# First attention: three VectorE steps move behind the next row's maxima, one ScalarE step moves ahead of two copies

## The reference, cut to what matters

```python
def _L0_xattn_ref(hidden_states, memory_tokens, memory_mask):     # (4,256,256), (4,1601,256), (4,1601)
    scores = jnp.einsum('bsd,bmd->bsm', hidden_states, memory_tokens) * scale
    scores = jnp.where(memory_mask[:, None, :], scores, neg_inf)
    attn = jax.nn.softmax(scores, axis=-1)
    readout = jnp.einsum('bsm,bmd->bsd', attn, memory_tokens)
    valid_b = jnp.any(memory_mask, axis=-1)
    return jnp.where(valid_b[:, None, None], readout, jnp.zeros_like(readout))
...
x = x + _L0_xattn_ref(_layernorm(x, axis=-1), ctx_2048, mask_BxS2_bk0)
```

## Time and profile before

| | us |
|---|---|
| median of 3 runs (their span) | 754.48 (749.64 to 755.35) |
| the profiled execution, whole | 752.55 |
| its span in the trace | 749.9 |
| TensorE busy in the span | 690.0 (92%) |
| VectorE busy | 536.6 (72%) |
| ScalarE busy | 396.5 (53%) |
| GpSimd busy | 174.7 (23%) |

### The profile page before, as it was taken

How to read it: one execution, slowest core, us unless ns; L and a number is a source line. 1 busy time by engine, 2 the same in 40 slices (tenths; PEclk the granted TensorE clock), 3 DMA queues, 4 the chain that set the end, 5 groups by cost and what they waited for, 6 DMA issues and landing times.

```text
span 749.9 us, 14907 instructions
## 1 busy us (share of the span) xinstructions
PE 690.0 (92%) x5499; PEld 533.7 (71%) x5499; DVE 536.6 (72%) x1174; ACT 396.5 (53%) x564; POOL 174.7 (23%) x220
## 2 busy tenths in 40 slices
PE   4899999997989999999999699999999999989990
PEld 4799899997778888888887454454455454677870
DVE  5766666677576666666666788789888878775655
ACT  2633332343322222322223699999999999533550
POOL 5462625240010000000000050003203604542651
PEclk9999999999999999999999999999999999899995
DMA  7357485822728766777669959986969750474545
GB/s 250 124 182 251 136 289 152 300 93 99 225 51 290 231 221 214 240 254 234 217 211 203 129 86 188 170 128 96 214 103 197 120 68 2 149 267 133 160 132 189
DMA packets 55211, 131.14 MB, mean 175 GB/s; under 512 B 10112, under 2 KB 36096, under 8 KB 51568
## 3 DMA queue, kind: packets, MB, share of 16 engines
q1 hardware_dynamic: 51888, 122.93, 61.9%
q0 software_dynamic: 2256, 6.18, 2.4%
q10 hardware_dynamic: 1008, 1.25, 0.5%
HBM read 78.78 MB, written 48.79 MB: 170 GB/s over the span
## 4 chain that ended last, share of the span: by engine, by line
PE 61%; ACT 11%; issue 10%; DVE 10%; DMA 4%; POOL 2%; SPq 0%; POOLq 0%; DVEq 0%; ACTq 0%
PE ps L657 14%; PE ps L658 14%; PE ps L659 14%; ACT p L1439 7%; PE ps L1001 5%; PE ps L1189 4%; PE ps L959 3%; PE ps L1205 2%; PE ps L1023 1%; DMA raw<-in_ctxN 1%; ACT cNh L1268 1%; PE ps L741 1%; PE ps L1173 1%; DMA raw<-in_ctxT 1%; DMA comb_b<-comb_rows 1%
## 5 line engine op out<-in xcount | busy, mean ns | idle before, releaser
L1439 ACT ACTIVATE p<-ps,kbias 128x1024 f32<-128x1024 f32 (+1 forms) x208 | 211.0, 1154 | 5.8 <-PE ps L959 5.7
L1951 DVE TENSOR_SCALAR p<-p 128x1024 f32<-128x1024 f32 (+1 forms) x208 | 140.7, 689 | 25.5 <-ACT p L1439 23.8
L1001 PE MATMUL ps<-p,vsl 128*17 128x256 f32 (+1 forms) x1664 | 114.2, 383 | 2.1 <-DVE p L1951 1.0
L1344 ACT ACTIVATE hh<-h 128x512 fp32r<-128x512 f32 x50 | 31.6, 632 | 132.6 <-DVE h L1818 115.5
L959 PEld LDWEIGHTS ps<-qst,kst 48*128 48x128 f32 (+1 forms) x832 | 58.7, 182 | 60.3 <-ACT p L1439 31.4
L959 PE MATMUL ps<-qst,kst 48*128 48x256 f32 (+1 forms) x832 | 91.0, 318 | 5.7 <-DVE qst L1894 1.6
L360 POOL TENSOR_SCALAR nv<-mv 128x2 f32<-128x2 f32 x8 | 6.8, 849 | 358.1 <-DVE mv L1881 210.7
L657 PE MATMUL ps<-xTh,w_hi 128*128 128x512 f32 x200 | 79.9, 400 | 1.5 <-DVE h L1814 0.8
L658 PE MATMUL ps<-xTl,w_hi 128*128 128x512 f32 x200 | 79.3, 397 | 0.0
L659 PE MATMUL ps<-xTh,w_lo 128*128 128x512 f32 x200 | 78.9, 395 | 0.0
L1001 PEld LDWEIGHTS ps<-p,vsl 128*17 128x17 f32 (+1 forms) x1664 | 35.8, 96 | 40.2 <-issue 7.4
(11 more groups left out here) (308 smaller groups left out, 1538.3 us busy)
## 6 DMA issues: line engine op xcount, KB each, us to landing
x_slots<-blank SPq DMA_DIRECT2D x20, 1032.0 KB, 5.9
kst<-k_hi SPq DMA_DIRECT2D x64, 200.2 KB, 8.9
w_raw<-in_w SPq DMA_DIRECT2D x25, 384.0 KB, 3.5
v_one<-vst SPq DMA_DIRECT2D x4, 1768.0 KB, 10.0
vsl<-v_one SPq DMA_DIRECT2D x4, 1768.0 KB, 17.0
kst<-k_lo SPq DMA_DIRECT2D x32, 200.2 KB, 8.9
raw<-in_ctxN SPq DMA_DIRECT2D x12, 512.0 KB, 5.7
e_w<-in_w SPq DMA_DIRECT2D x2, 3072.0 KB, 15.9
```

What stands on the lines that cost most here:

```text
L1001: mm = pe.matmul(ps[32 * j:32 * j + VW, 6 + job % 2, 0:SEQ], vsl[0:rows, b % 2, at_:at_ + VW], p32[0:rows, x % PBUF, (2 * t + c) * SEQ:(2 ...
L1344: act.activation(hh[:, half, :], h32[:, half, :], ACT.Copy).then_inc(hh_rdy, 1)
L1439: act.activation(p32[0:rows, x % PBUF, :], psf[0:rows, bank * 512:bank * 512 + 1024], ACT.Exp, scale=0.25, bias=kbias[0:rows, col:col + 1] ...
L1951: dve.tensor_scalar(t, t, CLO, CHI, ALU.max, ALU.min).then_inc(p_clip, 1)
```

## The change

Four edits, none of which adds or removes an instruction:

1. VectorE: `any_key(b)` moves from the even row to the odd one, behind `row_max`. `row_scale(i)` is cut in two: the reciprocal (`row_sum`) stays, the multiplication by `valid` moves behind the next row's `row_max`. `norm_lo(b + 1)` moves from the end of the even row to behind the odd row's `row_max`.
2. ScalarE: `norm_hi(b + 1)` moves ahead of `nat_hi(b, 2)` and `nat_hi(b, 3)`.
3. SyncE: `load_t(b + 1, 0)` and `load_t(b + 1, 1)` are issued ahead of `masks_in(b + 1)`.
4. After the last row one `row_scale(NI - 1)` follows.

```diff
--- before.py
+++ after.py
@@ -447,8 +447,10 @@
                 load_n(b, 2)
                 load_n(b, 3)
                 if b + 1 < NB:
+                    for k in range(2):
+                        load_t(b + 1, k)
                     masks_in(b + 1)
-                    for k in range(4):
+                    for k in range(2, 4):
                         load_t(b + 1, k)
                 for n in range(4, 8):
                     key_out(b, n)
@@ -1313,10 +1315,10 @@
                 pth(i, 2)
                 pth(i, 3)
                 if h == 0:
+                    if b + 1 < NB:
+                        norm_hi(b + 1)
                     nat_hi(b, 2)
                     nat_hi(b, 3)
-                    if b + 1 < NB:
-                        norm_hi(b + 1)
             if stop == "A":
                 return
 
@@ -1618,10 +1620,13 @@
                 dve.wait_ge(rscale_rdy, 2 * i + 2)
                 dve.scalar_tensor_tensor(out=resid[:, i, :], in0=ps[:, PVB, 0:D], scalar=rscale[:], in1=resid[:, i, :], op0=ALU.mult, op1=ALU.add).then_inc(R_ev, 1)
 
-            def row_scale(i):
+            def row_sum(i):
 
                 dve.wait_ge(exp_rdy, i + 1)
                 dve.reciprocal(rsum[:], psum_[:]).then_inc(rscale_rdy, 1)
+
+            def row_scale(i):
+
                 dve.wait_ge(rscale_rdy, 2 * i + 1)
                 dve.tensor_scalar(rscale[:], rsum[:], valid[:, 0:1], None, ALU.mult).then_inc(rscale_rdy, 1)
 
@@ -1665,6 +1670,12 @@
                     dve.wait_ge(bkv_in, 32)
                 if last:
                     next_stat(0, 3)
+                if h and b + 1 < NB:
+                    norm_lo(b + 1)
+                if h:
+                    any_key(b)
+                if i:
+                    row_scale(i - 1)
                 klo(b, h)
                 klo(b, h + 1)
                 if i:
@@ -1690,15 +1701,12 @@
                 vev(b, h)
                 ptl(i, 3)
                 vev(b, h + 1)
-                if h == 0:
-                    any_key(b)
-                row_scale(i)
+                row_sum(i)
                 for n in range(h + 2, h + 4):
                     vev(b, n)
-                if h == 0 and b + 1 < NB:
-                    norm_lo(b + 1)
                 if h and b + 1 < NB:
                     masks(b + 1)
+            row_scale(NI - 1)
             next_stat(NT - 2, NT - 1)
             for q, bank in enumerate((SB0, SB0 + 1, TB0)):
                 next_lo(q, bank)
```

## The result

| | before | after |
|---|---|---|
| median, us | 752.93 (749.64 to 757.19, 20 runs) | 756.62 (749.87 to 758.97, 20 runs) |
| profiled execution, us | 752.55 | 757.5 |
| its span, us | 749.9 | 754.9 |
| mean granted clock | 0.977 | 0.972 |

The ratio is 1.0046, with a 95% interval from 1.0032 to 1.0061. The changed kernel is slower by half a per cent. The prediction was a gain of 0.8 us; it is a loss of 3.7 us in the medians.

A forecast was written before the change was run, and what follows sets the result against it. TensorE, busiest in the first attention, waited 3.9 us on VectorE's bias addition; GpSimd's last split lay close behind. Batches lose 0.02, gain 0.38 and 0.42: 0.8 us, profiled 752.55 to 751.8, or 753.7 from the median; range 749.2 to 757.5.

The forecast's parts named there:

- VectorE's edits: Odd rows 1, 3, 5: TensorE's three waits on VectorE's bias addition before chunk 2 go, first-order gain 3.87 us.
- What is moved in front of `klo` costs nothing: VectorE, odd rows: 2.6 us moved ahead of `klo` is covered by 2.28 us idle and an earlier `nmax`; cost nothing.
- ScalarE's edit: `norm_hi` ahead of the natural copies: batch 0's copy and GpSimd's chain 0.96 us late, batches 1 and 2 no delay.
- SyncE's edit: Mask load waits for `any_key` until 85.1 us, hidden by 2.8 us before the third `load_t`; no gain from earlier loads.
- The sum: Even rows' start: TensorE, arriving sooner, waits for GpSimd's last split, so only 0.8 us of 3.87 is gained.
- A rule and a row: Mask bias starts at 95.58 inside GpSimd's last piece, stretches by up to 0.5 us, ends near 97.1, hidden.
- the terms of batches 1 and 2: First scores of rows 4 and 6 start after GpSimd's split, gaining 0.38 and 0.42 us.
- rival 2: Bias starts before GpSimd's last piece; GpSimd and TensorE stand still 0.98 us; 2.2 us lost, 756.7; chance 0.12.
- Rivals 1 and 3: 1: waits go, nothing replaces them, 750.6, chance 0.12; 3: VectorE still late by another wait, 754.5, chance 0.06.

The follow-up runs named there:

- the kernel without the meeting: The changed kernel, with VectorE's mask bias waiting for GpSimd's last split of the next batch's context: 751.99 us, ratio 0.9989.
- the filler: Twelve unread 400-column matmuls ahead of TensorE's wait for the last split, here added to kernel 13, where split and bias start together: 754.83 us, ratio 1.0018.
- the wait by chunk: The changed kernel, but an even row's scores wait for GpSimd's last split pieces only before chunk 2, the first that reads them: 748.47 us, ratio 0.9946.
- 13: The changed kernel, with GpSimd's last split also waiting for the VectorE instruction ahead of the bias, so both start together: 758.2 us, ratio 1.0061.
- 14: Kernel 13 plus twelve unread 400-column matmuls on TensorE ahead of its wait for the last split: 754.83 us, ratio 1.0018.
- 16: Kernel 13, with TensorE's wait for the last split moved from the first score chunk of rows 2, 4 and 6 to chunk 2: 748.17 us, ratio 0.9936.
- fifth: The changed kernel, with even rows' scores waiting for the last two context pieces only before chunk 2: 748.47 us, ratio 0.9946.
- eighth: The changed kernel without SyncE's edit, the mask load again ahead of all four `load_t`: 783.52 us, ratio 1.0428.
- the eleventh: The changed kernel, with VectorE's bias waiting for GpSimd's last high copy, ahead of the split: 752.67 us, ratio 1.0023.
- third: The changed kernel, with VectorE's bias waiting for GpSimd's last split of the next batch's context: 751.99 us, ratio 0.9989.
- seventeenth: Kernel 13, but the bias waits for the split's end, so the split starts as late and they never overlap: 755.97 us, ratio 1.0032.

## Why the prediction was wrong

**VectorE's edits** were right: all three waits on the addition went. The 3.87 us were under-sized: the odd rows' steps shrank by 4.72. What made the other 0.85 I haven't traced.

**What is moved in front of `klo` costs nothing**: right. In the changed kernel `any_key` stands at 83.29 (1.81 us) and the first `klo` at 85.26, with no TensorE wait behind it in any row, and the odd steps kept their full gain. The recorded rows had no `any_key` beside a GpSimd operation. Here there is one: it overlaps GpSimd's high copy of 84.42 us, and both take what they took before, 1.81 and 1.04 us.

**ScalarE's edit**: right in the profile. The natural copy started at 37.15 us in batch 0 (I had 36.82, against 35.86), and at 77.33 in batch 1 (77.30). The split of batch 0 ended at 55.63 for 55.69, and row 2 started at 55.73 for 55.71.

**SyncE's edit**: right. The mask load went at 85.12 (I had 85.1) and the third `load_t` at 87.97 (87.98). That the other order would have cost 27 us I had not seen.

**The sum**: the idea that GpSimd's last split bounds the even rows and takes most of the gain back was right, and the kernel without the meeting, at 0.9989, fits that sum. In batch 0 it held to 0.02 us: 0.92 lost in the even row where I had 0.94.

**The step that failed is "A rule and a row"**, and with it the terms of batches 1 and 2 in the sum. I let the bias start at 95.58, inside the last split, stretch by up to 0.5 us and stay hidden. It started at 95.31, and it was GpSimd that stood still. Two numbers in it were off. First the margin: 0.68 us forecast, 0.34 measured (95.31 against 94.97). Counted from row 2's exponential the bias came 0.21 us sooner than I had, since TensorE was 1.77 us quicker in row 3 and not 1.48, and the split 0.13 later; that is the missing 0.34. Then the point from which it decides: rival 2 had it at the split's recorded start, and the runs put it about a third of a microsecond behind (table below). The one row that I had the earlier trace rows was of a bias that came 1.51 us after GpSimd's start and couldn't show it. It held a sign that I passed over: GpSimd's operation there took 2.26 us, and one of the same shape takes 1.21 alone, so GpSimd too can be the one that is stretched.

**Rival 2 is what happened**, in two batches of three. I had given it 0.12 and 756.7 us; the median is 756.62. That the number fits is luck. It was reached from a median of three runs, 754.48, with a loss of 2.2 us; before has a median of 752.93 in twenty runs, and the loss is 3.7. The terms differ too. It took 0.6 and 0.56 us in batches 1 and 2 and 1.0 in batch 0; the split in fact cost its own stretch, 2.38 - 1.21 = 1.17 and 1.98 - 1.21 = 0.77, in batches 1 and 2 and nothing in batch 0, and the fall of the clock in row 4, 22.42 - 20.95 = 1.5 us against the same row with the filler, was in no case of mine. Against the forecast, rows 4 and 6 lost 4.13 + 2.71 - (1.10 + 1.05) = 4.7 us more. The stretch is 1.94 of it and the clock 1.5. Another 0.8 is that even a split of 1.21 us would have ended 1.25 and 1.67 us after TensorE's arrival and not 1.08 and 1.03; 0.5 of that mirrors the larger gain in rows 3 and 5 (GpSimd's end doesn't move with TensorE), and the rest is batch 2, where the split came later. TensorE's start 0.10 and 0.09 us behind the split, where I had 0.02, is 0.15, and 0.3 I can't place.

**Rivals 1 and 3** fell: the gain wasn't kept, and the waits didn't stay. Rival 1's outcome can be had, though, by the wait by chunk.

**The range** (749.2 to 757.5) held the median. I had put "within 1%" at 0.93, and it is within 1%. The sign was wrong, and with twenty runs of each kernel the interval lies clear of 1.

## What to carry to other kernels

When an edit moves an operation of VectorE earlier, look which GpSimd operation it now falls beside, and treat a margin below half a microsecond between the two starts as undecided: order the two, or move one to another engine. When a wait that is freed only reappears on the next semaphore, ask whether that semaphore is awaited earlier than its data is read: here one wait moved by two chunks turned a change of +0.5% into one of -0.5%. And a new wait of TensorE may cost more than its length, since the clock may fall behind it.

## What the runs showed of the hardware that I had not expected

**Who stands still.** "Lead" is the bias's start less the split's recorded start, in us. Alone the split takes 1.21 and the bias 0.98 to 1.00. All leads at which the bias and GpSimd's last split of a batch overlapped in the profiled executions (-0.22 stands for the nine meetings of kernels 13, 14 and 16, at -0.22 or -0.23):

| lead | stretched | to |
|---|---|---|
| 0.93, 0.94, 0.88, 0.83, 0.82, 0.80, 0.75 | bias | 1.13, 1.12, 1.19, 1.23, 1.24, 1.27, 1.31 |
| 0.62, 0.54, 0.51, 0.50, 0.42 | bias | 1.45, 1.52, 1.54, 1.55, 1.64 |
| 0.37, 0.31 | bias | 1.70, 1.74 |
| 0.34, 0.21, 0.14, 0.04, -0.03, -0.07, -0.22 | split | 2.38, 2.26, 2.19, 2.10, 2.01, 1.98, 1.82 or 1.83 |

In these 29 meetings it is one or the other and never both in part. The side changes at a lead of 0.31 to 0.37, where both happened. A stretched split ends 1.05 to 1.08 us after the bias, a stretched bias 0.84 to 0.86 after the split. The changed kernel's 0.34 lies on the edge, which fits its runs from 749.87 to 758.97 us, although the kernel before spreads by 7.5 too. The bias that meets GpSimd's high copy goes the same way: the copy is stretched at leads of 0.04 and 0.20 (to 1.92 from 1.04 and to 1.70 from 0.67), the bias at 0.45 and 0.61 (to 1.45 and 1.28; fifth and eighth kernel). So does the bias of batch 0 at the program's head, where it meets another split: the split is stretched at -0.10 to -0.08 (six kernels), the bias at 1.51 to 1.55 (twelve).

The Trainium skill, SBUF — State Buffer, section Who interferes with whom, says that the one which issues first has the shared pair for the whole instruction. By that rule the trace agrees, if "first" isn't read off the start that the profile records for GpSimd: with a lead of 0.04 to 0.34 the split has the earlier record and loses. The Trainium skill, Perfetto Trace Analysis, section GPSIMD Engine Instruction, warns that GpSimd's spans in a profile are unreliable; here the recorded start is off by a steady amount, if the rule holds: about a third of a microsecond, worked out from the lead at which the side changes.

**The clock.** The same wait doesn't always have the same effect. Ahead of the first scores of rows 2, 4 and 6, of eight waits of 2.52 or 2.53 us (changed kernel, the one without ScalarE's edit, the eleventh, the thirteenth) the clock fell behind five. Of four of 1.85 to 1.92 us (third and seventeenth kernel) it fell behind two. Row 7 has a wait of 1.90 to 1.93 us for `vst` in all eighteen kernels, which no edit touches; it fell right behind eight of those. Behind waits of 1.5 us and less, in the kernel before and in the experiments, it didn't. Why it fell behind one wait and not behind its equal stays open.
